# Expert results of a two-layer MoE kernel: four weighted rows per token, summed at the end, against scatters that add into two accumulators

## The reference

```python
x = x + attn_a(layernorm(x))          # x: (4, 512, 256) f32, causal, rotary
x = x + ffn(layernorm(x))             # layer "f" below
x = x + attn_b(layernorm(x))          # differential attention
x = x + ffn(layernorm(x))             # layer "h" below, the same weights
...
def ffn(x):                           # E = 16 experts, TOPK = 4, INTER = 176
    scores = softmax(xt @ Wg.T)
    topi = top_k(scores within the best 2 of 4 groups, 4)
    combine = zeros.at[t, topi].add(scores[t, topi])
    h = silu(xt @ W1[e].T) * (xt @ W3[e].T)
    y = sum over e of (h @ W2[e].T) * combine[:, e]
    z = silu(xt @ Ws1.T) * (xt @ Ws3.T) @ Ws2.T
    return y + z
```

## Time and profile before

| | |
|---|---|
| median of 3 runs | 1401.45 us (1400.99 to 1403.34) |
| the profiled execution | 1401.47 us, span 1399.7 us |
| PE, DVE busy | 1195.3 us (85%), 929.3 us (66%) |
| ACT, POOL busy | 555.8 us (40%), 571.3 us (41%) |
| granted TensorE clock, mean | 0.926 of full |
| bytes moved by DMA | 158.83 MB |
| `y_tok` stores, mean of one on POOL | 160, 959 ns |
| expert loops, first to last result issued | 471.6 to 667.5 us and to 1357.6 us |

### The profile page before, as it was taken

The page is one execution under the profiler, slowest core; times in us unless marked ns, Lnnn a source line. Parts: engine busy times, 40 slices in busy tenths (PEclk is TensorE's granted clock), DMA queues, the critical chain, the costliest instruction groups (busy, mean ns, idle before and its releaser), DMA issues.

```text
span 1399.7 us, 25657 instructions
## 1 busy us (share of the span) xinstructions
PE 1195.3 (85%) x8822; PEld 701.8 (50%) x8822; DVE 929.3 (66%) x2069; ACT 555.8 (40%) x922; POOL 571.3 (41%) x813
## 2 busy tenths in 40 slices
PE   6888999998899899999367899999868989999970
PEld 2343444433755577777133344444246547777750
DVE  5688898962672355555688799999376624555538
ACT  2125777777311222222121477777933112222210
POOL 4453343443037573343132355454610566633330
PEclk9988999999799899999788899999986999999995
DMA  4424333201712453332643322111070134433326
GB/s 142 136 83 132 114 114 117 92 22 71 277 43 106 139 164 108 108 108 79 248 135 113 126 59 60 53 55 49 3 290 27 71 119 144 149 108 107 108 91 266
DMA packets 107421, 158.83 MB, mean 113 GB/s; under 512 B 17248, under 2 KB 83616, under 8 KB 106784
## 3 DMA queue, kind: packets, MB, share of 16 engines
q1 hardware_dynamic: 92768, 117.89, 26.5%
q0 software_dynamic: 13824, 38.29, 7.4%
q10 hardware_dynamic: 704, 1.02, 0.2%
HBM read 87.87 MB, written 68.49 MB: 112 GB/s over the span
## 4 chain that ended last, share of the span: by engine, by line
PE 59%; DVE 22%; POOL 6%; ACT 6%; issue 5%; DMA 2%; SPq 0%; ACTq 0%; POOLq 0%; DVEq 0%
PE pair_ps L1682 14%; PE pair_ps L1695 10%; PE o_ps L1484 9%; POOL x_slots L548 5%; DVE x_sb L1044 4%; ACT arena L689 4%; DVE nm L939 4%; DVE bm L939 3%; PE pair_ps L1689 3%; PE t_ps L1510 2%; PE pair_ps L1434 2%; PE pair_ps L1414 2%; PE pair_ps L1439 2%; PE pair_ps L1315 2%; PE pair_ps L1337 2%
## 5 line engine op out<-in xcount | busy, mean ns | idle before, releaser
L689 ACT ACTIVATE arena<-pair_ps 128x1024 f32<-128x1024 f32 x320 | 322.8, 1025 | 129.4 <-PE pair_ps L1409 74.3
L508 POOL TENSOR_SCALAR_AFFINE_SELECT arena<-arena 128x512 f32<-128x512 f32 (+1 forms) x320 | 174.1, 544 | 248.7 <-ACT arena L689 248.7
L939 DVE TENSOR_REDUCE nm<-pair_ps 128x2 f32<-128x1024 f32 (+1 forms) x192 | 232.8, 1222 | 31.2 <-PE pair_ps L1458 27.1
L554 POOL DMA_INDIRECT y_tok<-xnT,dest x160 | 153.4, 959 | 210.9 <-DVE xnT L1223 150.0
L1682 PE MATMUL pair_ps<-arena 128*128 x640 | 220.3, 467 | 1.7 <-ACT arena L736 1.7
L548 POOL DMA_INDIRECT x_slots<-y_sb,slot_i x128 | 123.1, 961 | 177.2 <-DVE slot_i L1131 138.1
L1484 PE MATMUL o_ps<-arena 128*9 128x512 f32 (+7 forms) x2048 | 175.9, 438 | 4.0 <-POOL arena L508 4.0
L1695 PE MATMUL pair_ps<-arena 128*128 x640 | 164.4, 379 | 1.2 <-DVE arena L1216 1.2
L1211 DVE TENSOR_TENSOR arena<-arena,pair_ps 128x176 f32<-128x176 f32 x160 | 54.1, 338 | 160.1 <-ACT arena L741 160.1
L939 DVE TENSOR_REDUCE bm<-pair_ps 128x8 f32<-128x1024 f32 x128 | 155.4, 1218 | 6.0 <-PE pair_ps L1458 2.6
L1695 PEld LDWEIGHTS pair_ps<-arena 128*128 128x128 f32 x640 | 120.6, 190 | 44.5 <-issue 9.8
(11 more groups left out here) (208 smaller groups left out, 1731.5 us busy)
## 6 DMA issues: line engine op xcount, KB each, us to landing
arena<-x_slots SPq DMA_DIRECT2D x160, 132.0 KB, 2.3
arena<-y_tok SPq DMA_DIRECT2D x12, 1024.0 KB, 7.2
arena<-in_w SPq DMA_DIRECT2D x4, 2816.0 KB, 17.3
x_slots<-hw SPq DMA_DIRECT2D x20, 528.0 KB, 3.0
arena<-in_w SPq DMA_DIRECT2D x4, 2048.0 KB, 18.0
arena<-q_a SPq DMA_DIRECT2D x64, 96.0 KB
arena<-q_b SPq DMA_DIRECT2D x64, 96.0 KB
y_sb<-y_tok SPq DMA_DIRECT2D x4, 1024.0 KB, 14.1
```

The costliest lines, as they stand in the source:

```text
L508: pool.affine_select(p, p, pattern, ALU.is_ge, 0.0, base=0, channel_multiplier=-1)\
L554: pool.indirect_dma_start(y_tok, bass.IndirectOffsetOnAxis(ap=dest[:, j:j + 1], axis=0), yt[:, j % XR, :], None).then_inc(sm(f"store{j % X ...
L689: act.activation(p_ring[:, U % RING, :], pair_ps[:, pair_at("T", n, u)].rearrange("p a c -> p (a c)"), ACT.Exp, scale=SCALE).then_inc(sm(" ...
L939: dve.tensor_reduce(dst, src, X, ALU.max, negate=not 2 <= u < 4).then_inc(sm("t_max_done"), 1)
```

## The change

`y_tok` and its 8192 rows are gone. Each layer has two accumulators in DRAM, `y_acc[f][0]` and `y_acc[f][1]`, with one row per token (2048, and 512 for empty lanes). `y_sb` rows now carry the four slot numbers, the four weights and one row number (`EW` = 265), and `where` gives `slot_w`, the weight of each slot, and `dest`, its token. VectorE multiplies with `slot_w` when it evacuates. Result j is scattered with addition into accumulator j % 2; as the same token can stand in tile j and in tile j - 2, its issue waits until the scatter of j - 2 has landed. Accumulator 0 starts as `x_sb` with the shared expert added (`store_x`, four stores), accumulator 1 as zeros; the zeros and the spare rows are written in the first attention by 12 transfers of 512 KB. At the end SyncE loads both accumulators by batches, one into `x_sb` and one into `back`, and VectorE adds them, one operation a token tile.

```diff
-EW = E + 2 * TOPK
-ROWS = NT * P * TOPK
-PAIRS = NT // 2
-KEPT_PAIRS = 6
+EW = E + 2 * TOPK + 1
+ROWS = NT * P
+ACCS = 2
...
-        y_tok = nc.dram_tensor("y_tok", (ROWS + XR * P, E), F32).ap()
+        y_acc = {f: [nc.dram_tensor(f"y_{f}{a}", (ROWS + XR // ACCS * P, E), F32).ap() for a in range(ACCS)] for f in "fh"}
...
@@ -371,6 +370,11 @@
                 if s == "a" and n < NJ // 4:
                     sp.dma_start(x_slots[n * 4 * P:(n + 1) * 4 * P, :].rearrange("(a p) e -> p a e", p=P),
                                  zero.unsqueeze(1).to_broadcast([P, 4, EW])).then_inc(sm("slots_clear"), 16)
+                if s == "a" and n < 12:
+                    f, a = "fh"[n % 2], 0 if n < 2 else 1
+                    first = ROWS if n < 2 else (n // 2 - 1) * 4 * P
+                    sp.dma_start(y_acc[f][a][first:first + 4 * P, :].rearrange("(a p) e -> p a e", p=P),
+                                 zero[:, 0:E].unsqueeze(1).to_broadcast([P, 4, E])).then_inc(sm("acc_clear"), 16)
...
@@ -391,12 +395,21 @@
             def load(row, q):
                 sp.dma_start(xg[:, q, :], x_slots[ds(row, P), :]).then_inc(sm(f"load{q}"), 16)
 
+            def store_x(b):
+                sp.wait_ge(sm("e_z_free"), TB * (b + 1) + past(f, NT))
+                sp.dma_start(y_acc[f][0][b * T:(b + 1) * T, :].rearrange("(t p) e -> p t e", p=P),
+                             x_sb[:, b * TB:(b + 1) * TB, :]).then_inc(sm("acc_x"), 16)
...
             sp.wait_ge(sm("e_order"), 1 + past(f, 1))
+            for b in range(B - 1):
+                store_x(b)
             sp.wait_ge(sm("scat0"), 16 * EARLY_T * TOPK * (1 + past(f, 1)))
             for j in range(NJ):
+                if j == 4:
+                    store_x(B - 1)
...
@@ -409,12 +422,10 @@
 
             for q in range(XR):
                 sp.wait_ge(sm(f"store{q}"), 16 * (NJ // XR) * (1 + past(f, 1)))
-            rows = y_tok[0:ROWS, :].rearrange("(t p k) e -> p t (k e)", p=P, k=TOPK)
-            for n in range(PAIRS):
-                if n >= KEPT_PAIRS:
-                    sp.wait_ge(sm(f + "_x"), 2 * (n - KEPT_PAIRS) + 2)
-                sp.dma_start(back[n % KEPT_PAIRS].rearrange("p t k e -> p t (k e)"), rows[:, 2 * n:2 * n + 2, :])\
-                    .then_inc(sm(f"load{n}"), 16)
+            for b in range(B):
+                for a, to in ((0, x_sb), (1, back)):
+                    rows = y_acc[f][a][b * T:(b + 1) * T, :].rearrange("(t p) e -> p t e", p=P)
+                    sp.dma_start(to[:, b * TB:(b + 1) * TB, :], rows).then_inc(sm(f"load{2 * b + a}"), 16)
...
@@ -551,8 +562,14 @@
             def result_out(j):
                 pool.wait_ge(sm("e_dest"), j // 4 + 1 + past(f, NJ // 4))
                 pool.wait_ge(sm("e_y_ev"), j + 1 + past(f, NJ))
-                pool.indirect_dma_start(y_tok, bass.IndirectOffsetOnAxis(ap=dest[:, j:j + 1], axis=0),
-                                        yt[:, j % XR, :], None).then_inc(sm(f"store{j % XR}"), 16)
+                if j == 0:
+                    pool.wait_ge(sm("acc_clear"), 16 * 12)
+                    pool.wait_ge(sm("acc_x"), 16 * B * (1 + past(f, 1)))
+                if j >= ACCS:
+                    i = j - ACCS
+                    pool.wait_ge(sm(f"store{i % XR}"), 16 * (i // XR + 1 + past(f, NJ // XR)))
+                pool.indirect_dma_start(y_acc[f][j % ACCS], bass.IndirectOffsetOnAxis(ap=dest[:, j:j + 1], axis=0),
+                                        yt[:, j % XR, :], None, compute_op=ALU.add).then_inc(sm(f"store{j % XR}"), 16)
...
@@ -1036,14 +1053,10 @@
         def dve_back(dve, f, t):
 
 
-            for k in range(TOPK):
-                if k == 0:
-                    dve.wait_ge(sm(f"load{t // 2}"), 16 * (LOADS + past(f, LOADS)))
-                else:
-                    dve.wait_ge(sm("summed"), (TOPK - 1) * t + k + past(f, (TOPK - 1) * NT))
-                dve.scalar_tensor_tensor(x_sb[:, t, :], back[t // 2 % KEPT_PAIRS][:, t % 2, k, :], top[:, t, k:k + 1],
-                                         x_sb[:, t, :], ALU.mult, ALU.add)\
-                    .then_inc(sm("summed") if k < TOPK - 1 else sm(f + "_x"), 1)
+            if t % TB == 0:
+                for a in range(ACCS):
+                    dve.wait_ge(sm(f"load{2 * (t // TB) + a}"), 16 * (LOADS + past(f, LOADS)))
+            dve.tensor_tensor(x_sb[:, t, :], x_sb[:, t, :], back[:, t, :], ALU.add).then_inc(sm(f + "_x"), 1)
...
                 ch(dve.tensor_reduce(slot_f[:, half], mine, X, ALU.add))
                 ch(dve.tensor_scalar(y_sb[:, half, E:E + TOPK], slot_f[:, half], 1.0 + past(f, NJ * P), None, ALU.add))
+                ch(dve.tensor_copy(y_sb[:, half, E + TOPK:E + 2 * TOPK], top[:, half, 0:TOPK]))
                 dve.tensor_copy(slot_i[:, half, :], slot_f[:, half]).then_inc(sm("e_slots"), 1)
...
@@ -1220,7 +1234,8 @@
                 dve.wait_ge(sm("e_y_mm"), j + 1 + past(f, NJ))
                 if j >= XR:
                     dve.wait_ge(sm(f"store{j % XR}"), 16 * (j // XR + past(f, NJ // XR)))
-                dve.tensor_copy(yt[:, j % XR, :], st_ps[:, j % 2, 512:512 + E]).then_inc(sm("e_y_ev"), 1)
+                dve.tensor_scalar(yt[:, j % XR, :], st_ps[:, j % 2, 512:512 + E], slot_w[:, j:j + 1], None, ALU.mult)\
+                    .then_inc(sm("e_y_ev"), 1)
...
@@ -1235,11 +1250,13 @@
                                          slot_id[:, 4 * i:4 * i + 4].unsqueeze(2).to_broadcast([P, 4, TOPK]), ALU.is_equal))
                     ch(dve.tensor_tensor(where_k[:], where_k[:], xm[:, q:q + 4, 1, :], ALU.mult))
                 elif piece == 1:
-                    ch(dve.tensor_reduce(n[:, 0, :], where_k[:], X, ALU.add))
-                    ch(dve.scalar_tensor_tensor(n[:, 1, :], n[:, 0, :], 0.0, nowhere[:, q:q + 4], ALU.is_equal, ALU.mult))
+                    w = slot_w[:, 4 * i:4 * i + 4]
+                    ch(dve.tensor_reduce(w, where_k[:], X, ALU.add))
+                    ch(dve.scalar_tensor_tensor(n[:, 0, :], w, 0.0, nowhere[:, q:q + 4], ALU.is_equal, ALU.mult))
                 elif piece == 2:
-                    dve.scalar_tensor_tensor(dest[:, 4 * i:4 * i + 4], n[:, 1, :], -1.0, n[:, 0, :], ALU.add, ALU.add)\
-                        .then_inc(sm("e_dest"), 1)
+                    w = slot_w[:, 4 * i:4 * i + 4]
+                    ch(dve.scalar_tensor_tensor(n[:, 1, :], w, 0.0, x_row[:, q:q + 4], ALU.is_gt, ALU.mult))
+                    dve.tensor_tensor(dest[:, 4 * i:4 * i + 4], n[:, 0, :], n[:, 1, :], ALU.add).then_inc(sm("e_dest"), 1)
...
@@ -1738,9 +1755,8 @@
         np.tile((i4[None, :] < i4[:, None]).reshape(1, -1), (P, 1)),
         np.tile((i16[None, :] < i16[:, None]).reshape(1, -1), (P, 1)), 
         np.tile(np.concatenate([np.arange(16) * P, np.arange(NJ), i16])[None, :], (P, 1)),
-        ROWS + 1 + P * np.arange(XR)[None, :] + r[:, None],
-        TOPK * (P * np.arange(NT)[None, :, None] + r[:, None, None]).repeat(TOPK, 2).reshape(P, -1)
-        + np.tile(i4 + 1, NT)[None, :],
+        ROWS + P * (np.arange(XR)[None, :] // ACCS) + r[:, None],
+        P * np.arange(NT)[None, :] + r[:, None],
```

More of the change, by code:

```diff
@@ L61 @@
 EARLY = 24
-assert (ROWS + NE * (P - 1)) // P <= NJ <= P and NJ % XR == 0 and PAIRS == XR
+assert (ROWS * TOPK + NE * (P - 1)) // P <= NJ <= P and NJ % XR == 0 and XR == 2 * B
 assert EARLY * P <= EARLY_T * P * TOPK - NE * (P - 1)
@@ L113, in build @@
         xg = arena[:, o_g:o_w].rearrange("p (q e) -> p q e", q=XR)
-        xm = xg[:, :, E:EW].rearrange("p q (a k) -> p q a k", a=2)
+        xm = xg[:, :, E:E + 2 * TOPK].rearrange("p q (a k) -> p q a k", a=2)
+        x_row = xg[:, :, E + 2 * TOPK]
         xgT = arena[:, o_w:o_w + 512].rearrange("p (a c t) -> p a c t", a=2, c=CE)
@@ L152, in build @@
         yt = xnT2[:, :, :, :].rearrange("p a c t -> p (a c t)").rearrange("p (q e) -> p q e", q=XR)
-        c_f = sb("c_f", [P, 128 + 16 + 256 + 16 + NJ + 16 + XR + NT * TOPK + 4])
+        c_f = sb("c_f", [P, 128 + 16 + 256 + 16 + NJ + 16 + XR + NT + 4])
         c_b = sb("c_b", [P, 128 + 256 + 256 + 256], BF16)
@@ L162, in build @@
         y_flat = y_sb[:, :, :].rearrange("p t e -> p (t e)")
-        back = [arena[:, o_p + 2 * TOPK * E * n:o_p + 2 * TOPK * E * (n + 1)] for n in range(4)]
-        back += [y_flat[:, 2 * TOPK * E * n:2 * TOPK * E * (n + 1)] for n in range(2)]
-        back = [a.rearrange("p (t k e) -> p t k e", t=2, k=TOPK) for a in back]
+        back = arena[:, o_p:o_p + NT * E].rearrange("p (t e) -> p t e", t=NT)
         sil = sb("sil", [P, 2, T])
@@ L189, in build @@
         slot_id = sb("slot_id", [P, NJ])
+        slot_w = sb("slot_w", [P, NJ])
         first_row = sb("first_row", [P, NJ], I32)
@@ L217, in build @@
         nowhere = c_f[:, o:o + XR]
-        rows_i = c_f[:, o + XR:o + XR + NT * TOPK].rearrange("p (t k) -> p t k", t=NT)
-        o += XR + NT * TOPK
+        rows_i = c_f[:, o + XR:o + XR + NT]
+        o += XR + NT
         lane, lane_late = c_f[:, o:o + 1], c_f[:, o + 1:o + 2]
@@ L1053, in dve_ffn @@
```

(2 more changed lines are left out.)

## The result

The changed kernel takes 1387.96 us (median of 4 runs, 1386.70 to 1390.0) beside 1401.93 for the kernel before (4 runs, 1400.99 to 1403.34): ratio 0.9901, interval 0.9884 to 0.9918. It is 14 us faster where 36.4 were forecast. 1388 lies in the stated 1357 to 1394, in the part above 1377 that stood for the rivals A and C, not for the forecast.

What follows compares the result with a forecast made beforehand. TensorE was taken to bound the expert loop, and VectorE, loads and output the tails. Second tail -17.2, first tail -20.1, added work +0.4 and +0.5 gave -36.4: 1365 us from 1401.45, range 1357 to 1394 (forecast's own 1357 to 1377).

Steps and rivals of the forecast that it cites:

- A: Rival: tails shrink by less or the expert loop is a little slower, 1376 to 1399 us; chance 0.11 together with C.
- C: Rival: GpSimd's scatter issue grows from 0.96 us; at 2.0, 10.4 us lost per layer, 1386; chance 0.11 together with A.
- Second tail: After the second expert loop: smaller loads and plain adds end the kernel at 1382.5 us, 17.2 us earlier.
- T: Issue of SyncE's first load back in a tail, forecast to come 1.1 us later in both tails.
- First tail: After the first expert loop: cheaper VectorE adds and a vanished TensorE stall save 20.1 us.
- my upper bound: Most the first tail could save: 26.6 us, sixteen times 1.54 and the two stretched dve_back calls.
- The adding store: Expert loop: result j waits for j-2's landing; hidden up to two tiles, 4.97 us; tails start 1.1 us later.
- The landing: Time for an adding result scatter to land: taken as 3.5 us, estimate 3.0 to 4.8, plain 2.42.
- L: Landing of an adding store; beyond 4.64 us GpSimd doesn't catch up, beyond 5.2 it eats what a tail saves.
- Rival B: Adding stores handle rows one after another, 0.39 us a row passing a 5.2 us landing; 1456 to 1790 us; chance 0.16.
- Engine time: DMA engines in the loop: an adding store takes 0.70 us of each; share about 52%, no bound.
- Added work: Outside the tails: assign copy 0.4 us, clears and storing x_sb zero, longer rows and VectorE work 0.5; upper bound 3.

Runs made afterwards that it cites:

- plain_no_add: Changed kernel with result scatters writing instead of adding, every wait kept: 1361.21 us, ratio 0.9701 to the kernel before.
- four_sums: Changed kernel with four accumulators instead of two, only two loaded back, clears behind the first attention: 1378.27 us, ratio 0.9828 to the kernel before.
- rows_left_out: Changed kernel without the 20 row scatters between results and SyncE's wait for them: 1361.35 us, ratio 0.9707 to the kernel before.
- four_sums_rows_ahead: Changed kernel with four accumulators, two loaded back, and 52 row scatters ahead of result 0: 1357.79 us, ratio 0.9685 to the kernel before.
- clears_behind: Changed kernel with its 12 accumulator clears moved out of the first attention's slots, behind the last move of maxima: 1391.97 us, ratio 0.9916 to the kernel before.
- rows_ahead: Changed kernel with 52 row scatters instead of 44 ahead of result 0: 1385.08 us, ratio 0.9867 to the kernel before.
- add_in_before: Kernel before, its result scatters adding into cleared y_tok, rows all different, no result waiting for another: 1422.1 us, ratio 1.0137 to the kernel before.
- third_sum: Changed kernel with three accumulators for results 0 to 47, 52 row scatters ahead, clears behind attention: 1368.64 us, ratio 0.9757 to the kernel before.

## Why the prediction was right and wrong

**Second tail: right.** 18.3 us were forecast from the first load back to the end, 18.8 came: end at T + 20.8 (forecast T + 21.3), first addition at T + 5.4 (5.3).

**First tail: mechanism right, size too small.** Forecast 21.2 from T, measured 28.4, 0.7 beyond my upper bound (26.6 and 1.1). `xn` starts 10.9 us after T (forecast 11.2, before 17.0). TensorE's second eight matmuls show the stall of 5.44 us gone:

```profile
708.91 3.70 PE L1354 MATMUL pair_ps<-xnT,wqkv 128*128 128x512 f32 x8 [0.21 <-DVE arena L836]
```

They start 21.7 us after T where it was 32.9, 11.2 earlier, as forecast (10.1 and 1.1). What was too small is the rest, 17.2 instead of 10.0, and most of that is the clock. The stretch from `xn` to the clearing of `o_ps`, before and after:

```profile
687.00:790.00 103.00, 72.90 (x382) 38.44 (x384) 86.35 (x164) 23.28 (x69) 28.34 (x35) 0.85 0.42 140
```

```profile
698.00:778.50 80.50, 64.25 (x380) 35.23 (x380) 67.59 (x127) 23.67 (x69) 27.77 (x35) 0.97 0.52 165
```

The same matmuls take 64.25 us of TensorE instead of 72.90, since the granted clock is 0.97 instead of 0.85: 8.65 us that the sum didn't have, for it took TensorE's work as a constant. How much of it the time got back can be read from the other runs, for the same tail ran there at lower clocks too, in plain_no_add:

```profile
686.00:769.00 83.00, 67.72 (x380) 36.61 (x380) 67.58 (x126) 23.67 (x69) 27.80 (x35) 0.91 0.52 159
```

From T to the clearing of `o_ps` the tail lasts 91.1 to 91.8 us in the four kernels with a clock of 0.97 in this stretch (changed, four_sums, rows_left_out, four_sums_rows_ahead), 93.0 at 0.94 (clears_behind), and 94.1 and 94.6 at 0.91 (plain_no_add, rows_ahead). That is 3 us for 0.057 of the clock; carried on to 0.85, my estimate is 6 of the 7.2 us.

**The adding store: the step that failed.** The sum kept GpSimd's issue at 0.96 us ("GpSimd's issue grows" was rival C, and with A it had 0.11) and moved each tail by 1.1 us. The issue is 1.56 us. C's mechanism happened: 48.4 us for twelve results, the ring of eight full, the 64th row scatter late for row load 24. Why an adding issue is longer, by C's third address or otherwise, no run shows. Until result 8 the results are 4.47 us apart, which is GpSimd's queue without a pause: 1.62, 0.98 and 0.96 us of issues with 0.30 between. I had worked C out at 2.0 us as a ring stall of 6.7 us and a lag of 3.7; at 1.56 the ring cost 3.8 (1.4 of it by my estimate the longer landing), the late row load 4.4, and the lag 4.9 and 7.5. C's 10.4 a layer became 13.5 and 15.6. By C's own working 1.56 us would have cost only 1.4 a layer: 17.8 behind, 16.4 allowed, and a gain of 0.63 a result until GpSimd is level. Two things were missing in it: the late row load was named but given no price, and C was worked out without the chain, which cut that gain to 0.05 to 0.08 a result. The longer issue alone makes the loss in the loop (add_in_before); the lag at the end needs it and the chain together, and each was priced as if the other didn't happen.

Four tests agree on the loop: add_in_before has its loss without the chain, plain_no_add doesn't have it, rows_ahead and rows_left_out remove it with the add in place, with its landing and its load on the engines.

**The landing: right as a landing, wrong as a period.** I took L = 3.5 and said that beyond 4.64 GpSimd doesn't catch up. The median landing is 3.8 us, 0.3 off. But the chain's period is from issue to issue, 4.87 us (rows_ahead): the mean landing of 4.04, 0.76 until GpSimd issues again, and what it is late by itself. The plain store has the same 0.76: in plain_no_add, results 12 and 14 are issued at 516.53 and 519.73, 3.2 us apart, where the landing is 2.42. So 4.64 was passed and GpSimd didn't catch up, as the threshold said: four_sums shows the lag that it costs, third_sum gets most of it back. 5.2, from which it would eat what a tail saves, was not passed, and rows_left_out shows a chain that costs nothing. So the term for the landing itself was right (1.1 us, measured 1.4 and 1.2); the lag of 4.9 and 7.5 that the chain carries was put at nothing.

**Rival B fell.** It asked for 0.39 us a row and more, and a landing above 5.2; 128 rows land in 3.8 us, and a row takes 0.14 us of its engine (1.09 below, by eight).

**Engine time.** 43.3% of 198 us less 20 row scatters at 0.35 us leave 78.7 us for 72 result scatters, 1.09 us of each engine, 3.1 times the plain 0.35. "Collectives: The Full Stack" of the Trainium skill, section "The bandwidth ceiling: the fold count and why AG ≠ RS ≠ AR", says of ReduceScatter that the add's second read halves the rate, by estimate twice the engine time; here it is three times. I had said that it is no bound, and rows_left_out bears that out (0.66 of the engines, TensorE 99.86 of 100).

**Added work.** The clears were put at nothing because one slot of SyncE was free. In the slots ahead of a move of maxima they were not hidden: 2.2 us. The copy in `assign` is 0.2 us in the first layer (from the first FFN weight load to the first row scatter 63.1 us, before 62.9), as forecast. The fourth store of x and the 1060-byte rows cost nothing in the loop (plain_no_add), though `L1237` takes 484 ns where the copy took 425.

**Sum.** The tails gave 7.7 us more than forecast, the work up to the last landing took 30.1 more: -36.4 + 30.1 - 7.7 = -14.0.

## What to carry to other kernels

When a store waits for an earlier one, count the period from issue to issue (issue, landing and the engine's own restart), and compare it with the time of the work between: a period just under it costs nothing until the engine is once late, and then it lets it catch up by hardly anything (3 to 5 us in a loop of 196 here). When an instruction on a queue grows, add up the queue's work over its busiest stretch, not its mean, and go through every buffer and every load that waits behind it. Work the rivals out together as well as one by one: here either of the two alone left GpSimd level at the end (add_in_before, rows_left_out). A cure for the first wait can hand its whole gain to the second; run the cures together before judging either.

## What was not expected of the hardware

An indirect store with addition takes GpSimd 1.56 us to issue (0.96 plain, 128 rows of 1 KB), lands after 3.8 us in the median (2.4 plain), up to 5.2 for single ones, and takes 1.09 us of each DMA engine (0.35 plain). From a landing to the issue that waited for it 0.76 us pass, with the add and without. And in the first tail TensorE's granted clock was 0.97 where it was 0.85 (2.4 GHz is the full level, 1.2 the lower), in a stretch in which it waits less for VectorE. That the shorter waits caused it is not shown: all runs of the new tail are above 0.85, but with the same instructions in it they have 0.91, 0.94 or 0.97.
